# A three-stage mixer on one core: VectorE's constant scalars from columns, a split in four steps, halves folded into weights, and redrawn orders

## The reference

```
y  = moe(layernorm(x))                         # one of 8 experts for each token
s  = attention(layernorm(x)) @ out_w + out_b
x1 = x + s * y * sigmoid(y)      # kernel: 0.5*(tanh(y/2) + 1)*y*s
pool = xn.reshape(64, 8, 128).mean(1)          # latents of B
gk, gv = pool @ wgk, pool @ wgv
s  = (gated local + gated remote attention) @ w_out
o  = transformer(xn)             # q and k divided by their norms, clipped at 1e-12
out = x1 + s * o * sigmoid(o)
```

## Time and profile before

| | |
|---|---|
| median of 3 runs | 3473.93 us (3471.63 to 3474.02) |
| profiled execution, its own time | 3440.83 us |
| its span | 3439.0 us |
| PE busy | 3112.3 us, 90% |
| DVE busy | 2466.9 us, 72% |
| ACT busy | 2338.7 us, 68% |
| POOL busy | 1261.4 us, 37% |

### The profile page before, as it was taken

One profiled execution on the slowest core, in us unless ns is written; L12 is line 12 of the kernel. 1 busy time (PEld: TensorE's weight loads), 2 busy tenths in 40 slices (PEclk: granted clock), 3 DMA queues, 4 the chain that ended last, 5 costly groups with the idle time before them and its releaser, 6 DMA issues.

```text
span 3439.0 us, 83502 instructions
## 1 busy us (share of the span) xinstructions
PE 3112.3 (90%) x34007; PEld 1889.5 (55%) x34008; DVE 2466.9 (72%) x5000; ACT 2338.7 (68%) x4758; POOL 1261.4 (37%) x799
## 2 busy tenths in 40 slices
PE   5589799999999999999999999999999999999976
PEld 5168445556564646555565656565555656464644
DVE  6432487868687877878676868778786868687643
ACT  1265467777777786777767776867777777778744
POOL 1622034333333443444333333444443333344343
PEclk9889899999999999999999999999999999999987
DMA  6256110101011111101011111111010101111000
GB/s 190 69 160 187 48 28 14 32 27 38 27 28 31 34 31 34 31 16 33 23 36 29 28 31 34 31 34 31 15 35 22 38 27 28 34 31 31 5 13 4
DMA packets 130458, 138.95 MB, mean 40 GB/s; under 512 B 17972, under 2 KB 112542, under 8 KB 129566
## 3 DMA queue, kind: packets, MB, share of 16 engines
q1 hardware_dynamic: 120368, 104.77, 11.2%
q0 software_dynamic: 9712, 28.85, 2.9%
HBM read 80.87 MB, written 35.39 MB: 34 GB/s over the span
## 4 chain that ended last, share of the span: by engine, by line
PE 46%; DVE 21%; ACT 9%; POOL 6%; issue 4%; DMA 2%; SPq 2%; POOLq 0%; ACTq 0%; DVEq 0%
PE bank L1882 5%; PE bank L1319 4%; DVE turn_f L2056 4%; PE bank L698 4%; PE bank L1926 3%; ACT prob_a L1388 3%; PE bank L1303 3%; PE bank L1332 3%; DVE nmax_a L1443 3%; PE bank L1868 3%; PE bank L1858 2%; PE bank L1849 2%; DVE ss L2049 2%; DVE nmax_f L2063 2%; POOL turn_f L1797 2%
## 5 line engine op out<-in xcount | busy, mean ns | idle before, releaser
L1388 ACT ACTIVATE prob_a<-bank 128x512 f32<-128x512 f32 x1024 | 564.4, 607 | 190.0 <-PE bank L1332 185.2
L1443 DVE TENSOR_REDUCE nmax_a<-bank 128x1 f32<-128x512 f32 x768 | 502.5, 684 | 161.6 <-PE bank L1303 160.5
L1791 POOL TENSOR_TENSOR rn<-ss,minus_half 128x16 f32<-128x16 f32 x128 | 377.8, 2952 | 270.6 <-DVE ss L2051 268.6
L1814 POOL TENSOR_TENSOR rs_f<-rs_f,minus_half 128x4 f32<-128x4 f32 x32 | 32.6, 1018 | 1108.2 <-DVE rs_f L1181 1108.2
L1797 POOL TENSOR_TENSOR turn_f<-turn_f 128x512 f32<-128x512 f32 x256 | 324.3, 1287 | 207.7 <-DVE turn_f L2056 207.7
L1332 PE MATMUL bank<-Qst_a,Kst_a 74*128 74x512 bf16 x1024 | 378.9, 389 | 18.9 <-ACT prob_a L1388 9.5
L1944 ACT ACTIVATE area<-bank 128x512 f32<-128x512 f32 x640 | 349.9, 603 | 63.2 <-PE bank L1882 55.2
L2056 DVE TENSOR_TENSOR turn_f<-area,rotf 128x1024 f32<-128x1024 f32 x256 | 307.6, 1219 | 8.7 <-POOL area L1801 6.2
L1303 PE MATMUL bank<-Kst_a,Qst_a 72*128 72x512 bf16 x768 | 302.2, 394 | 5.4 <-DMA Kst_a<-dk_a 1.2
L1319 PE MATMUL bank<-prob_a,V_a 128*9 128x512 f32 x2048 | 274.5, 609 | 13.2 <-ACT prob_a L1388 11.8
L1801 POOL TENSOR_TENSOR area<-turn_f,rn 128x1024 f32<-128x1024 f32 x128 | 267.5, 2090 | 19.0 <-POOL turn_f L1797 0.9
(11 more groups left out here) (288 smaller groups left out, 7007.4 us busy)
## 6 DMA issues: line engine op xcount, KB each, us to landing
Qst_a<-dq_a SPq DMA_DIRECT2D x192, 96.0 KB
Kst_a<-dk_a SPq DMA_DIRECT2D x192, 96.0 KB
dq_a<-prob_a SPq DMA_DIRECT2D x80, 128.0 KB
dk_a<-prob_a SPq DMA_DIRECT2D x48, 128.0 KB
area<-xs_d SPq DMA_DIRECT2D x39, 128.0 KB, 4.3
ys_d<-otok_f SPq DMA_DIRECT2D x39, 128.0 KB, 1.9
x_a<-in_x_in SPq DMA_DIRECT2D x16, 256.0 KB, 2.8
xs_d<-turn_f SPq DMA_DIRECT2D x4, 1024.0 KB, 9.9
```

The costliest lines, as they stand in the source:

```text
L1388: nc.scalar.activation(dst, bk.full(act, product)[0:rows, :], func, **kw).then_inc(a_emptied["act"], 1)
L1443: nc.vector.tensor_reduce(out=nmax_a[:, g, t, j:j + 1], in_=bk.full(dve, f)[:], op=ALU.max, axis=AX.X, negate=True).then_inc(emptied, 1)
L1791: nc.gpsimd.tensor_tensor(rn[:, t % 2], ss[:, t % 2], minus_half[:], ALU.pow).then_inc(f_root, 1)
```

## The change

Two [128, 1] tiles are set once: `one_c` holds 1.0 and `tiny_c` holds 1e-24. Instructions that had a constant in the instruction now read it from such a column: the limit of L2051, and the 1.0 of the gates. The casts of `split_max` become multiplications by `one_c`. The split's last two steps become one subtraction that writes bf16. The factor 0.5 of both gates is multiplied once into `bo0`, `wo0_s` and `w_out_s` in the opening, and the factor 1/8 of the mean into `blocks_l` and into the copy of `V_l`.

```diff
+            for half in (bo0, wo0_s):
+                last = nc.vector.tensor_scalar(half[:], half[:], 0.5, None, ALU.mult)
+            link(last)
...
+                    nc.vector.tensor_scalar(blocks_l[:], blocks[0:NL, 0:LH], 1.0 / POOL, None, ALU.mult)
+                    nc.vector.tensor_scalar(w_out_s[:], w_out_s[:], 0.5, None, ALU.mult)
...
-            link(nc.vector.tensor_tensor(res, res, parts[1], ALU.subtract))
-            yield at + 0.4
-            nc.vector.tensor_copy(parts[2], res).then_inc(inc, 1)
+            nc.vector.tensor_tensor(parts[2], res, parts[1], ALU.subtract).then_inc(inc, 1)
...
-            link(nc.vector.tensor_copy(mhi, nmax))
-            nc.vector.tensor_copy(parts[0], mhi)
+            link(nc.vector.tensor_scalar(mhi, nmax, one_c[:, 0:1], None, ALU.mult))
+            nc.vector.tensor_scalar(parts[0], mhi, one_c[:, 0:1], None, ALU.mult)
...
-            link(nc.vector.scalar_tensor_tensor(out=th_a[:], in0=th_a[:], scalar=1.0, in1=y_a[:], op0=ALU.add, op1=ALU.mult))
+            link(nc.vector.scalar_tensor_tensor(out=th_a[:], in0=th_a[:], scalar=one_c[:, 0:1], in1=y_a[:], op0=ALU.add, op1=ALU.mult))
...
-            nc.vector.scalar_tensor_tensor(out=x1_a[:]..., in0=th_a[:], scalar=0.5, in1=x_a[:]..., op0=ALU.mult, op1=ALU.add)
+            nc.vector.tensor_tensor(x1_a[:]..., th_a[:], x_a[:]..., ALU.add).then_inc(a_x1, 1)
...
-            link(nc.vector.tensor_reduce(out=pool_b[:], ...))
-            nc.vector.tensor_scalar(pool_b[:], pool_b[:], 1.0 / POOL, None, ALU.mult).then_inc(b_pool, 1)
+            nc.vector.tensor_reduce(out=pool_b[:], ...).then_inc(b_pool, 1)
...
-                last = nc.vector.tensor_copy(V_l[...], ps[...])
+                last = nc.vector.tensor_scalar(V_l[...], ps[...], 1.0 / POOL, None, ALU.mult)
...
-            nc.vector.scalar_tensor_tensor(out=x_f[:]..., in0=mix_f[:], scalar=0.5, in1=x_b[:]..., op0=ALU.mult, op1=ALU.add)
+            nc.vector.tensor_tensor(x_f[:]..., mix_f[:], x_b[:]..., ALU.add).then_inc(f_out, 1)
...
-                nc.vector.tensor_scalar(ss[:, t % 2], ss[:, t % 2], 1e-24, None, ALU.max).then_inc(f_sq, 1)
+                nc.vector.tensor_scalar(ss[:, t % 2], ss[:, t % 2], tiny_c[:, 0:1], None, ALU.max).then_inc(f_sq, 1)
...
-STEP = 177.9173333
+STEP = 179.028
...
             "finish": ((13.2, 13.4, 13.6),
-                       (-76.74182, -61.91878, -61.91678))}}
+                       (-90.50874, -89.91647, -62.32792))}}
```

More of the change, by code:

```diff
@@ L231 @@
             "b": ((1.3, 2.3),
-                  (-13.62627, -12.62627)),
+                  (46.03138, 47.03138)),
             "head": ((0, 9.5, 12, 17, 29.6),
-                     (-15.12171, 8.59514, 10.05181, 18.6592, 69.16135)),
+                     (-22.48616, 21.58838, 30.37351, 30.37551, 47.15188)),
             "f": ((0, 8.1, 14.2),
-                  (-76.6243, -60.87516, -48.15163)),
+                  (-62.80022, -39.22137, -37.20174)),
             "a": ((14, 34, 36, 56, 59, 83),
-                  (-117.93683, -108.734, -106.94609, -81.78519, -71.29696, -27.93752)),
+                  (-102.633, -102.631, -102.629, -75.32815, -68.3772, -58.13768)),
             "finish": ((14.7, 15.7),
-                       (-39.45796, -38.45796))},
+                       (-56.79986, -55.79986))},
         "gpsimd": {
             "gate": ((0, 1),
-                     (-47.04021, -46.04021)),
+                     (-59.02423, -58.02423)),
             "b": ((0.5, 1.5),
-                  (-4.97401, -3.97401)),
+                  (-29.35423, -28.35423)),
             "head": ((1, 2),
[1 row of a table removed]
[1 row of a table added]
             "f": ((5, 6.5, 10.4, 11.9, 15.8, 17.3, 21.2, 22.7, 47, 70, 71.5, 75.4, 76.9, 80.8, 82.3, 86.2, 87.7),
[2 rows of a table removed]
[2 rows of a table added]
             "feed": ((6.8, 7.8),
-                     (-115.0227, -114.0227))},
+                     (-136.08242, -135.08242))},
         "tensor": {
@@ L296 @@
                    101.2, 102, 102.4, 104, 105, 108, 110),
[20 rows of a table removed]
[20 rows of a table added]
             "feed": ((6.05, 6.425, 8.05, 8.55, 8.65, 9.05, 9.15, 9.55, 9.65, 9.7, 10.2, 10.7),
-                     (-119.98984, -114.2711, -106.73414, -103.91178, -103.90978, -103.90778, -103.90578,
-                      -103.90378, -103.90178, -103.89978, -100.51421, -93.56947))},
+                     (-121.61351, -116.42462, -110.63065, -108.80481, -108.80281, -108.31128, -105.53537,
+                      -105.53337, -105.53137, -105.35708, -102.41886, -98.24093))},
         "scalar": {
             "gate": ((112, 113),
[1 row of a table removed]
[1 row of a table added]
             "b": ((1, 2, 2.1, 2.2, 2.3, 2.4, 3, 3.2, 3.4, 6, 7, 7.4, 8, 8.4, 9, 9.4, 10, 10.4, 11, 11.4, 12,
                    12.4, 13, 13.4, 13.6, 14, 14.4, 15, 15.4, 16, 16.4, 17, 17.4, 18.4, 23, 24),
[4 rows of a table removed]
[4 rows of a table added]
             "head": ((4.6, 6.1, 29.05),
[1 row of a table removed]
[1 row of a table added]
             "f": ((1, 1.2, 1.4, 1.6, 1.8, 1.9, 2, 6.4, 6.6, 6.8, 7, 7.2, 7.3, 7.4, 11, 11.2, 11.8, 12, 12.2,
@@ L357 @@
                    96.4, 97.6, 98.8, 100, 101.2, 102.4, 104.6, 108),
[10 rows of a table removed]
[10 rows of a table added]
             "feed": ((6.175, 8.3, 8.55, 9.05, 9.55),
-                     (-119.82581, -107.55224, -103.59258, -103.40648, -101.00127)),
+                     (-121.1862, -111.21311, -107.23236, -105.93275, -103.55128)),
             "finish": ((11.2, 12.2),
-                       (-93.02697, -92.02697))},
+                       (-95.2636, -94.2636))},
         "vector": {
             "gate": ((113, 113.2, 113.4),
[1 row of a table removed]
[1 row of a table added]
             "b": ((0, 0.2, 0.5, 1.5, 2.6, 3, 3.2, 3.5, 5.1, 5.2, 5.3, 5.35, 7.1, 7.2, 7.3, 7.35, 9.1, 9.2, 9.3,
@@ L377 @@
                    15.2, 15.3, 15.35, 15.95, 17.95, 19.95, 22, 22.5),
[5 rows of a table removed]
-            "head": ((1, 1.2, 1.5, 6.2, 6.5, 6.6, 6.7, 6.8, 6.9, 16, 16.7, 17.4, 18.1, 18.8, 19.5, 20.2, 20.9,
[4 rows of a table removed]
[5 rows of a table added]
+            "head": ((1, 1.2, 1.5, 6.2, 6.5, 6.6, 6.7, 6.8, 16, 16.7, 17.4, 18.1, 18.8, 19.5, 20.2, 20.9, 21.6,
[4 rows of a table added]
             "f": ((4, 4.5, 5, 9.4, 9.9, 10.4, 13.6, 13.9, 14.8, 15.3, 15.8, 19, 19.3, 20.2, 20.5, 20.7, 21.2,
@@ L404 @@
                    98.4, 99.6, 100.8, 102, 103.5, 105, 111),
[10 rows of a table removed]
[9 rows of a table added]
             "feed": ((6.55, 6.8, 7.1, 8.8, 9.3, 9.8, 10.725),
-                     (-113.68945, -113.49199, -109.75291, -99.7432, -99.7412, -97.62405, -91.88652)),
+                     (-115.65749, -115.65549, -111.85462, -107.56182, -105.69138, -101.43757, -96.93134)),
             "finish": ((13.2, 13.4, 13.6),
-                       (-76.74182, -61.91878, -61.91678))}}
+                       (-90.50874, -89.91647, -62.32792))}}
 SEATS = {
-    "a": ("254203542054321052043524034510511415123514045345035030102525035230214135243515300531031003"
-          "4513421403035420250352105113200"),
-    "b": "331035134113500030533454325534522200",
[L423 to L426, removed]
+    "a": ("404230542054210431253021534010511435123514005340535101430532055230020135243511500513031035"
+          "2130122341213254350352542053210"),
+    "b": "110435144113500331510153325553320000",
+    "head": "51521204250415320345",
+    "f": ("150121023243051204031214321241421345024254050105210103524421423520342032053205420311232414"
+          "1032342014401421"),
+    "feed": "433045045"}
 B_AT = 5
@@ L640, in mixer_kernel @@
         minus_half = sb("minus_half", [P, 2 * FH])
+        one_c, tiny_c = sb("one_c", [P, 1]), sb("tiny_c", [P, 1])
+        blocks_l = sb("blocks_l", [NL, LH])
         stats_b, mv_b, rs_b = sb("stats_b", [P, NT, 6]), sb("mv_b", [P, NT, 2]), sb("rs_b", [P, 2, NT])
@@ L967, in open_vector @@
             nc.vector.memset(acc_b[:], 0.0)
+            nc.vector.memset(one_c[:], 1.0)
+            nc.vector.memset(tiny_c[:], 1e-24)
             for tile in (V_b[:], V_l[:], kT_b[:, :, 0:WIN], xnT_b[:, 0:WIN], x1_a[:]):
@@ L1482, in gate_vector @@
                 dve.wait_ge(*nth(r - 1, f_x_kept, 16))
-            nc.vector.scalar_tensor_tensor(out=x1_a[:].rearrange("p t e -> p (t e)"), in0=th_a[:], scalar=0.5,
-                                           in1=x_a[:].rearrange("p t e -> p (t e)"), op0=ALU.mult, op1=ALU.add).then_inc(a_x1, 1)
+            nc.vector.tensor_tensor(x1_a[:].rearrange("p t e -> p (t e)"), th_a[:], x_a[:].rearrange("p t e -> p (t e)"),
+                                    ALU.add).then_inc(a_x1, 1)
         def b_sync(r, sp, bk, beside_f, fk):
@@ L1703, in b_vector @@
             dve.wait_ge(*bk.brought("bxnT", "act"))
-            link(nc.vector.tensor_reduce(out=pool_b[:], in_=xnT_b[:, WIN:WIN + T].rearrange("p (l t) -> p l t", t=POOL),
-                                         op=ALU.add, axis=AX.X))
```

(14 more changed lines are left out.)

## The result

The changed kernel takes 3590.03 us in the median of 4 runs (3576.57 to 3601.94), against 3473.97 us for the kernel before on the same chip. The ratio is 1.0329, with a 95% interval of 1.0287 to 1.037. It is slower by 3.3%. The forecast was 3464 us with a range of 3420 to 3500, so the range does not hold it. The forecast also gave a gain a chance of one half. The trace is of the longest of the four executions.

The account below looks back on a forecast made before the run. The prediction took TensorE (PE), busy 95% of ten rounds, as the bound. Its terms summed to −0.7 us a round, −10.7 us over 15 rounds, and +0.5 once, giving 3464 us after scaling, range 3420 to 3500.

Parts of the forecast that it names:

- The new order: Instructions reordered on DVE and POOL: L2030 with L2034, gather and split change places; together to cost 1.8 us a round.
- the pair: L2030 and L2034, moved behind a turning ahead of group 2's maxima, delay those maxima: +2.6 us a round.
- the gather: On POOL, no longer between a scaled tile and the next power; one wait of L1824 goes: −0.2 us a round net.
- If the column form doesn't stall: On DVE, L1203 and L2051 reading a column no longer wait for POOL, giving back 2.24 us a round.
- rival: Instructions reading columns still stall behind POOL, so 1.9 us a round is not won: 3491 us; chance 0.20.
- Added by columns: 1.1 us.: Eighteen DVE instructions a round read a column, each 0.06 us longer: 1.1 us a round.
- Taken from DVE: L1706 and one cast of the split go, and stalls of L1203 and L2051 end: 4.0 us of DVE time a round.
- −0.55: L2030 leaves the place where it stalled behind POOL in some rounds: 0.55 us a round won.
- −0.46: The split is shorter and starts ahead of the turnings, so L1291's wait for its data goes: 0.46 us a round won.
- +0.4: L1193, in the split, stands nearer the turnings and is held longer by POOL: 0.4 us a round lost.
- The factor 0.85: Share of a DVE stall that reaches the round, measured at L2030 and used everywhere to turn DVE time into round time.

## Why the prediction was wrong

**Where the sum went wrong.** In us a round, by the ratios: the split and the halves were to bring 1.5 and brought 1.2. The columns were to bring 1.0 in the net (1.9 of stalls given back, 0.9 of added time) and cost 3.7. The new order was to cost 1.8 and cost 6.0. Two steps failed, each by over 4 us. A column was priced by its own length and by stalls it would end, without asking where POOL's next instruction starts. And the new order was priced too low at the pair and with the wrong sign at the gather, with no term for the clock.

**The bound and the stalls.** Right: PE bounds the kernel, DVE's work reaches it in part, and a stall on DVE is one of POOL's instructions seen from the other side. Each long stall shown above ends with an instruction of POOL.

**"If the column form doesn't stall."** This is a step that failed, and the forecast had its failure as a rival with a chance of 0.20. In the old order the first cast of the maxima stands 0.90 us with a column as without, and in the new one the limits stand up to 1.78. The gain of 2.24 us a round was never there. The rule of the Trainium skill (page "SBUF — State Buffer", section "Who interferes with whom"), that `tensor_scalar` can ask for the shared pair, without an exception for columns, agrees with the 0.90 of L1206.

**"Added by columns: 1.1 us."** The term that failed worst in its kind. Each column costs its 0.06 us, as the 235 for 174 ns show, but their effect on the round is not the sum. Ten of them cost 0.2%, which is what the forecast's 0.6 x 0.85 us a round makes. Eight in the maxima cost 1.4%, 48 us, 3.2 us a round, and a single one of each pair 1.3%: once a round one instruction stands 1.7 us more, and in the old order L2030 then stands 2.6 us in nearly every round. The row that held this was in the forecast's own timeline: L1205 and POOL's L1801 both start at 1988.10. The forecast read it as the end of one stall, and not as a start that had no room left. The rival was right that the column form stalls, and had nothing of the threshold: it left the columns at 0.9 us a round (1.1 x 0.85), where 1.6% or 3.7 us were measured.

**"Taken from DVE" without columns.** Right in size: 1.77 us x 0.85 x 15 is 23 us, 0.66%; measured 0.52% (0.34 to 0.70).

**The moved pair, "+2.6".** Right in place and sign, too small. Moving it back brings 1.6%, 55 us, 3.7 us a round without columns. The chain was right in part: L2036 stood 0.63 and not about 2.3 us, and L2040 0.35, but then the cast itself stood another 1.6 (1.5 with a column), which the forecast did not count. Together they delay the maxima by 2.2 us and not 3.0: PE takes them 5.7 us after the turning with the pair there and 3.5 without. All of it reaches PE, whose wait for the maxima is 2.2 us a round longer. So the place itself was priced too high rather than too low. What was missed is behind it: PE's busy time with the same matmuls is 1.6 us a round longer (1807.01 against 1791.50 us in ten rounds), and other waits 0.5 (4.3 in all in these ten rounds). The −0.55 for L2030 was not there: L2036 takes 1.38 us in nearly every round, where L2030's mean was 1.33. With columns the move back brings only 0.4 to 0.8%, and there the subtraction stands behind the threshold in two groups.

**The gather, "−0.2".** Wrong in sign. The wait of L1824 did fall, from 11.7 to 6.7 us in ten rounds, but not by the gather: without columns it is 5.7 with the gather in its new place and 5.8 with it moved back, and 12.0 once the pair is moved back. The four DMA issues now hold the next tile's additions by 3.4 us and bring them to the start of the maxima: 0.6%, 1.3 us a round, against the 0.4 that stood in the sum.

**The split's wait, "−0.46", and L1202.** The wait for the DMA is gone in the changed kernel, as said. L1202 became shorter (1.79 for 2.08), not longer; the cast behind it became longer (L1204, 2.35 for 1.67) and the last subtraction shorter (L1206, 1.22 for 1.95). The +0.4 was thus put on the wrong instruction, and the split as a whole is not held longer.

**The factor 0.85.** It was taken from a stall in a place with some room. At the moved pair, where PE waits already, the delay counts in full, and then the clock comes on top: in the changed kernel PE's busy time grew by 3.2 us a round though it had nothing more to do. The forecast had no term for the clock.

**The sum.** In per cent of the kernel before: split and halves −0.5, columns in the maxima +1.4, columns elsewhere +0.2, new order +2.6 (1.0208 over 0.9948), of it pair 1.6 and gather 0.6. Together 3.7, where 3.3 and 3.7 were measured on two chips. The parts depend on what they are measured beside: with the old instructions the new order costs 3.7, so there the split and the halves are worth 1.6 and not 0.5. What makes the last 0.5% of the new order was not tried. The waits name a candidate that neither move touches: L1838 for DVE's `prob_a`, 13 to 16 us in ten rounds of the new order without columns, is not among the waits of the old order.

## What to carry to other kernels

An instruction that shares a port with another engine has a price with a step in it: ask not how much longer an edit makes it, but when its neighbour on the other engine starts, and how much room there is, and what stands next once the order has shifted. Where two starts in a timeline agree within 0.1 us, take that as a cost that waits to happen. When work is put ahead of a small instruction that a bound engine waits for, count its own time and the stall that the small one then runs into. Edits that take instructions away from a stalled engine were worth their time by the rows; the new order hid that gain under a loss five times as large.

## What the runs showed of the hardware

- In the kernel before, the subtraction that begins with POOL's scaling, or 0.01 us after it, took 0.17 us in all 15 rounds (L1205's most is 0.172 in 64). With columns it begins 0.07 us after and took 1.88 in all 15. The Trainium skill (the page and section named above) says that whoever issues first has the pair for the whole instruction. The trace agrees for the subtraction at 0.07 us, but not to the letter: at up to 0.02 us behind POOL it still passed, and L2030 in the earlier trace rows began 0.22 us ahead of POOL's additions, in the last 0.24 us of POOL's power, and yet stood until both additions were through.
- L2036 and L2040, with both tensor inputs in SBUF, stood only 0.63 and 0.35 us while POOL's pair ran for 2.95, and POOL's pair was 0.46 longer: L2036 began 0.44 us into the first addition, stood until that one ended, and then ran its last 0.55 us while the second was held. So it came in between POOL's two additions, where L2030 stood for both (2.59). Why the one passes and the other doesn't was not tried.
- After PE stood for 2.27 us, the granted clock was at its lower level for some 7 us.
